# Layer zero's query weight issued ahead of the token rows on ScalarE's DMA queue, in a two-layer cross-attention kernel

## The reference

```python
# layer zero: 8 heads of 40, keys and values from three sets of 16 context rows
q       = heads(x @ w_q)
z_anat  = attend(q, heads(anat @ w_k),      heads(anat @ w_v))       # rows 16..31
z_dis   = attend(q, heads(dis @ w_k_dis),   heads(dis @ w_v_dis))    # rows 0..15
z_delta = attend(q, heads(delta @ w_k_dis), heads(delta @ w_v_dis))  # the last 16 rows
x       = merge(0.5 * z_anat + 0.5 * z_dis + z_delta) @ w_out + b_out + x
# layer one: 20 heads of 16 over all 1024 context rows
q, k, v = heads(x @ Wq), heads(ctx @ Wk), heads(ctx @ Wv)
x       = merge(softmax(q @ k.T / 4) @ v) @ Wo + bo + x
```

## Time and profile before

| | |
|---|---|
| three runs | 330.17, 330.56, 332.45 us (median 330.56) |
| span of the profiled execution | 329.9 us |
| PE busy | 314.6 us (95% of the span) |
| DVE busy | 263.2 us (80%) |
| ACT busy | 235.3 us (71%) |
| POOL busy | 75.6 us (23%) |
| moved by DMA | 27.92 MB, 85 GB/s on average |
| mean granted TensorE clock | 0.999 of full speed |

### The profile page before, as it was taken

The page is one execution under the profiler, slowest core; times in us unless marked ns, Lnnn a source line. Parts: engine busy times, 40 slices in busy tenths (PEclk is TensorE's granted clock), DMA queues, the critical chain, the costliest instruction groups (busy, mean ns, idle before and its releaser), DMA issues.

```text
span 329.9 us, 6007 instructions
## 1 busy us (share of the span) xinstructions
PE 314.6 (95%) x2030; PEld 166.2 (50%) x2030; DVE 263.2 (80%) x468; ACT 235.3 (71%) x488; POOL 75.6 (23%) x108
## 2 busy tenths in 40 slices
PE   8699999999999999999999999999999999999995
PEld 7377698866667633434333343343333454434324
DVE  2349799979887889999999999999999889892123
ACT  3527347343535797979878988899797978798982
POOL 5055246243426310010100100101041434102000
PEclk9999999999999999999999999999999999999999
DMA  7950007759996401905209064090350000000002
GB/s 226 304 198 0 2 2 192 208 165 190 170 251 199 141 21 55 143 4 100 46 8 139 1 90 58 5 140 1 78 70 1 3 21 24 21 2 22 3 0 80
DMA packets 15189, 27.92 MB, mean 85 GB/s; under 512 B 2839, under 2 KB 6967, under 8 KB 15159
## 3 DMA queue, kind: packets, MB, share of 16 engines
q1 hardware_dynamic: 14071, 26.41, 36.1%
q10 hardware_dynamic: 1088, 1.14, 1.2%
HBM read 18.19 MB, written 9.18 MB: 83 GB/s over the span
## 4 chain that ended last, share of the span: by engine, by line
PE 75%; DVE 14%; DMA 3%; ACT 2%; issue 2%; SPq 1%; ACTq 1%; POOL 1%; POOLq 0%
PE ps L1394 23%; PE ps L1371 16%; PE ps L1382 14%; PE ps L1191 12%; DVE mx L883 6%; PE ps L1006 3%; DMA cs<-in_ctx_dram 3%; PE ps L1228 1%; PE ps L1138 1%; ACT probs L662 1%; DVE d L832 1%; ACT q0T L590 1%; DVE max L828 1%; ACTq L286 1%; SPq L285 1%
## 5 line engine op out<-in xcount | busy, mean ns | idle before, releaser
L883 DVE TENSOR_REDUCE mx<-ps 128x1 f32<-128x512 f32 x320 | 198.9, 683 | 20.1 <-PE ps L1371 19.3
L662 ACT ACTIVATE probs<-ps 128x512 f32<-128x512 f32 x320 | 166.4, 607 | 27.8 <-PE ps L1382 25.8
L1394 PE MATMUL ps<-probs,VS 128*32 128x512 f32 (+1 forms) x696 | 86.7, 570 | 0.3 <-ACT probs L662 0.3
L1371 PE MATMUL ps<-KS,QS 48*128 48x512 f32 x256 | 84.2, 445 | 2.2 <-DVE mx L883 1.1
L1382 PE MATMUL ps<-QS,KS 50*128 50x512 f32 x256 | 80.3, 436 | 0.1
L1382 PEld LDWEIGHTS ps<-QS,KS 50*128 50x128 f32 x256 | 38.5, 185 | 36.8 <-ACT probs L662 28.8
L1371 PEld LDWEIGHTS ps<-KS,QS 48*128 48x128 f32 x256 | 38.2, 184 | 36.1 <-DVE mx L883 26.4
L539 POOL TENSOR_TENSOR attn<-o_turned,o_rec 128x256 f32<-128x256 f32 x9 | 5.6, 622 | 95.9 <-DVE o_rec L897 95.8
L1394 PEld LDWEIGHTS ps<-probs,VS 128*32 128x32 f32 x696 | 13.7, 108 | 25.8 <-ACT probs L662 16.0
L1371 PE MATMUL ps<-KS_last,QS_last 48*128 48x512 f32 x64 | 23.0, 444 | 1.1 <-DVE mx L883 1.0
L644 ACT CAST parts<-ps 128x512 fp32r<-128x512 f32 (+1 forms) x18 | 10.5, 585 | 18.7 <-PE ps L1191 16.1
(11 more groups left out here) (194 smaller groups left out, 439.3 us busy)
## 6 DMA issues: line engine op xcount, KB each, us to landing
KS<-k_parts SPq DMA_DIRECT2D x48, 128.0 KB, 4.3
k_parts<-parts SPq DMA_DIRECT2D x8, 512.0 KB, 3.2
QS<-q_parts SPq DMA_DIRECT2D x48, 64.0 KB, 4.5
q_parts<-parts SPq DMA_DIRECT2D x4, 512.0 KB, 2.9
cs<-in_ctx_dram SPq DMA_DIRECT2D x2, 768.0 KB, 10.1
KS_last<-k_parts SPq DMA_DIRECT2D x12, 128.0 KB, 4.2
xs<-in_x_dram SPq DMA_DIRECT2D x2, 640.0 KB, 7.1
out_dram<-xs SPq DMA_DIRECT2D x7, 160.0 KB, 1.8
```

The source lines that it names most:

```text
L662: act.activation(probs[:, t % 2 * GH + h, :], ps[:, bank_of["s", m], :], ACT.Exp, scale=float(D1) ** -0.5).then_inc(exp_done, 1)
L883: dve.tensor_reduce(mx[:, g % BUF, u:u + 1], ps[:, bank_of["m", n], :], AX.X, ALU.max).then_inc(max_done, 1)
L1371: pe.matmul(ps[:, bank, :], QS[g % BUF][rows, pair, qt * P:(qt + 1) * P], KS[g % BUF][rows, pair, half * 512:half * 512 + 512], start=True ...
L1394: m = pe.matmul(ps[2 * D1 * h:2 * D1 * (h + 1), bank_of["pv", g], cols], VS[:, g % 2, kt, h, :], probs[:, t % 2 * GH + h, cols], start=(kt ...
```

## The change

The loads of layer zero's query weight move from behind the three token DMAs to ahead of them in ACT's program. Nothing else is edited; the amount of data, the number of DMAs and the work of every engine stay as they were.

```diff
         @block.scalar
         def _(act):
+            load_weight(act, wq0, w_q0, P, wq0_in)
             for n, t0 in enumerate(SETS):
                 act.dma_start(tok[n * TOK:(n + 1) * TOK, :, :], ctx_768[:, t0:t0 + TOK, :].rearrange("b t n -> t b n")).then_inc(tok_in, 16)
-            load_weight(act, wq0, w_q0, P, wq0_in)
             act.wait_ge(id_ready, 1)
             act.activation(first_exp[:, :], ident_f[:, 0:1], ACT.Exp)
```

## The result

The changed kernel took 333.29 us (median; 331.78 to 333.71) beside 330.37 us for the kernel before. The ratio is 1.0068, with a 95% interval of 1.0040 to 1.0096. It is slower, by 2.9 us between the medians and by 0.7% in the ratio, and lies above the range of the prediction. Measured a second time beside other runs of the kernel before it came to 333.42 against 330.67 us, 1.0079 (1.0048 to 1.0109). Medians and ranges here are over all executions; a ratio leaves out those that took over 1.5% longer than the fastest of the same kernel.

What follows compares the result with a forecast made beforehand. The prediction took the start to be bound by `cs0` landing at 14.20 us, then PE's work. Terms of 0 on PE, 0 on ACT and DVE and -0.1 through `cs0` gave span 329.8, time 330.5 us, range 329.1 to 332.6.

Steps and rivals of the forecast that it cites:

- Cost on the path: 0: PE before `cT 0`: tokens 1.8 us late, all taken up by the waits for `wk`, `wv` and `cs0`.
- the clock: Rival: PE idle from about 6.3 to 8.0 us lowers its clock, some 4.2 us showing, time 334.7; chance 0.04.
- signs of being wrong: PE waiting for `tok` beyond 8.6, no `cs0` wait, clock below 1.00 in first 15 us, `cs0` over 0.5 us from 14.2.
- what bounds the start: Start of the kernel: chain through DMA `cs0`, landing at 14.20 us; later PE delay goes almost one for one into the end.
- The query weight had slack: Query weight's path to PE: split by 13.30, first read at 15.39, so 2.1 us to spare; gain 0.
- x of batch 0: First rows PE needs: landing about 1.1 us later, at 6.2 instead of 5.1, if `wq0` took half the engines; cost 0.
- The bounds of the token landing: Token DMAs: 6.8 us if the queue ahead costs nothing, 10.0 us as the last on q10.
- T: Moment the tokens land, set at 8.0 us from q10's bulk end, half a microsecond for landing and part of the tail.
- the cover: PE before `cT 0`: arriving at T + 5.6, lateness stays hidden up to T = 8.6; past that each microsecond costs one.
- The token rival: Tokens land after 8.6, so PE reaches `cT 0` behind `cs0`; 332.0 us at the upper bound of 10.0; chance 0.18.
- the offset: Conversion of profiled span to measured time: median 0.66 us above the profiled span, so 329.8 became 330.5 us.

Runs made afterwards that it cites:

- the kernel with the extra warm-up: Changed kernel plus a third warm-up of eight unneeded products ahead of the tokens, the second staying behind them; 331.78 us beside 330.31, ratio 1.0042.

## Why the prediction was wrong

**The step that failed** is "Cost on the path: 0". The late tokens were on the path and cost 1.5 us, and the clock, at nothing in the sum, cost 1.6. All of the prediction's signs of being wrong came: PE waited for `tok` until 9.2, no wait for `cs0` was left, the clock stood at 0.50 before 15 us, and `cs0` landed at 13.2, 1.0 us from 14.2.

**Right:** what bounds the start. PE's work from `cT 0` on is a constant to within 0.5 us, and the time moves one for one with it. The query weight had slack, and issuing it earlier gained nothing. x of batch 0 was not late: 4.1 us to landing in place of 4.3. I had allowed 1.1 us more, and the rule of the Trainium skill that I set beside it, page "DMA: Bandwidth & Descriptors", section "Queues, rings and completion order", would also have made it later; the trace shows no delay. The bounds of the token landing, 6.8 and 10.0, held what came.

**Wrong, the size of T.** I took 8.0; PE got the tokens at 9.22, and at 9.15 in the second trace. I had let q10's bulk end decide and taken little of the thin tail, though three small transfers need all their packets; that it was this tail is not shown. What is shown: the last token DMA was issued at 3.06 in place of 2.7, as each issue took about 0.54 us and not 0.45, and it took 6.1 us to landing where T = 8.0 left it 5.3.

**Wrong, the cover.** It was reckoned against `cs0` at 14.20, from one trace. With PE at `cT 0` 5.36 us after the tokens (I had 5.6), the cover of that execution ends at 8.8, but the usual execution, with `cT 0` near 13.1 by the estimate above, covers only to about 7.7. At 9.2 this makes 1.5 us, which is what the kernel with the extra warm-up shows. The token rival had the right mechanism, at 0.18, and its price was measured from the wrong end.

**Wrong, the clock.** This rival had 0.04 and came true in nine of ten executions. I argued that pauses of 0.94 and 1.19 us had not lowered the clock and that the new one was near in length. It was 2.1 to 2.4 in the two traces, about twice the longest. The row did not bear the step from one to the other. The price was the other way off: up to 4.8 us if the warm-up and both `kvp` units ran at half speed, where the clock was low for only 3.4 us and cost 1.58. By the Trainium skill, page "TensorE: Matmul & The Clock Gate", Part 1, an idle TensorE is throttled to half; the rows at 0.50 agree, and that warning was worth more than the chance I gave it.

**Wrong, the offset.** I put the median 0.66 us above the profiled span. In every execution whose span is listed the time lies about 1.7 us above it (333.59 with 331.9, 331.78 with 330.0). By that offset the profiled execution of before took about 331.6 us and was a late one, which the comparison of one span with the median of others hid.

In sum, with the two parts as the kernel with the extra warm-up separated them: 330.4 for the kernel before, + 1.5 for the tokens and + 1.6 for the clock make 333.5, against 333.29 and 333.42 measured.

## What to carry to other kernels

The transfer issued earlier on its queue made those behind it later here, by its issue time and by its bytes; ask first which of them the in-order engine reads next, and move only data that is next in line. Take the slack of a wait from several executions, since the landing that covers it can move by more than the slack. And price a pause of TensorE together with the work behind it: filling this one with further products that nothing needs won 1.5 us, and moving into it the second warm-up, which stood behind it, won all 3.

## What the runs showed of the hardware

In both traces of the changed kernel the clock fell although PE was busy again: 1.3 us after it had resumed, following a pause of 2.1 us, and 0.5 us after, following one of 2.4. It came back 3.4 us later, while the warm-up and then `kvp 0` ran. Without the second warm-up it fell as PE resumed or just before, at 9.2 and 9.4 us, and stayed at the lower level for 10 us, although PE is shown busy throughout from 10 us on, with both `kvp` units, the transposes of the context and the first query products.

In the two traces without the second warm-up, each the longest of its kernel, it fell again for 6.8 us at about 118.5 us. The longest wait of PE in the 58 us before was 0.8 us. A low mean clock therefore does not say that the start was the cause.

The granted clock at the very start can't be read from its column. It shows 1.00 from 0 us on in all traces, but the first matmuls take 421 ns, where the same form later takes 275. In the changed kernel's first trace the transposes of x still ran at that pace:

```profile
L1086 PE MATMUL ps<-ident_f,xs x8: 421/421/421, 5.2 to 6.7; 128*128 128x128 f32 x8
```

In the first trace of before their median was 273 ns. Between executions of one order of DMAs the same eight transposes took 1.09 to 1.7 us, which I read as a first rise of the clock at a different moment in each execution; no column shows it.

A 768 KB load, issued at 5.8 us beside the same other transfers, took 6.8 to 8.4 us to land in four traces with the tokens first. I had not expected a single large load to vary by 1.6 us.
